# Splits of units 3, 6 and 9 ahead of GpSimd's wait for the next mask; halved mask loads, a three-part bfloat16 turn, and inverse sums of two groups widened in DRAM

## The chip, the cores and the metric

The kernel runs on one core of one Trainium2 chip. The metric is the device time of one execution in microseconds, from the runs' median. The engines of the core are TensorE (PE, its weight loads are PEld), VectorE (DVE), ScalarE (ACT), GpSimd (POOL) and SyncE (SP), each with a queue of its own that it works off in order; transfers go through 16 DMA engines.

## The reference, cut to what matters

```python
x = layernorm(x + self_attention(x))          # 1024 tokens, 16 heads of 8, one key/value head
x = layernorm(x + cross_attention(x, ctx, mask))   # 6404 context rows, 16 heads of 8
x = layernorm(x + experts(x))                 # top-1 of 8 experts, 128 x 128 each

# in both attentions, per head (the cross one with masked scores at -1e9)
scores = q @ k.T / sqrt(8)
out = softmax(scores) @ v
```

All inputs are float32. The mask is int32, 1024 x 6404; where it is 0 the score becomes -1e9, and here that is the same columns for every token: all but a tail of the context.

## The kernel before

**Units and steps.** Each attention is cut into 16 units: 8 pairs of heads times 2 halves of the tokens (512 each). A unit of self attention has 8 steps, one of cross attention has 10 (`SELF_U`, `NBLK`; `X(j, b)` is block b of cross unit j). The kernel keeps 1280 keys for the cross stage: the last 1024 and one chunk of 256 that the mask leaves alive. One step of the main loop does, on TensorE: two "column" products of keys and queries into an ST bank (L1539 in self, L1752 in cross), two "row" products of queries and keys into an RT bank (L1527, L1745), 16 steps ahead of the columns, and the products of probabilities and values of the step before (L1512, eight small matmuls). DVE takes the maximum of each RT bank (L944, L961, L962); ACT makes the exponentials of ST (L1309, L1298). RT has two banks, ST three; they go round in the order of `RT_AT` and `ST_AT`, in which extra jobs (`RT_JOBS`, `ST_JOBS`) take a bank each.

**Maxima.** A softmax needs its row maxima before its columns. When a unit's last row is reduced, DVE writes its maxima to `finx` (L938). GpSimd splits them in `split_max` (L566, L568) into a high and a low float32r part, `mxh`. TensorE turns `mxh` by a matmul with the identity (`turn_max`, L1490) three or five steps ahead of where the unit's columns begin (`TURN`), ACT copies the result to `mxr` (L1238), and SP sends it as rows of `Qs` (`max_rows`, issue at L317), where it is subtracted within the column products. TensorE waits for the split at the turn, and for the landing at the unit's first column (`have_max`).

**The mask.** GpSimd counts the mask in 16 pieces m (128 tokens x 3328 columns of int32, 1.7 MB each). Per piece it waits for the load, clamps it to bytes (L613), adds it to the counts (L622) and asks for piece m + 2 (`load_mask`, issue at L543). The splits stand in the same queue at fixed places: `MAX_AHEAD` says which split comes before the clamp of a piece, and so before the wait for its load, `MAX_BETWEEN` which comes between clamp and add. From the counts DVE finds the live chunk, which the cross stage needs.

**Sums.** The values' matmuls also give each head's sum of exponentials. They go out with the outputs to DRAM and come back as `den`, and the outputs as `aTr` (`o_back` on SP). There are four groups: s0, s1 (self, first and second half of the tokens), x0, x1. DVE inverts `den` (`sums_back`, L1050). TensorE spreads the inverses to all rows of a head with a selecting matrix (`spread`, L1600, an RT job); DVE multiplies (`spread_rows`, L1056, into `aT`); TensorE projects (`project_out`, L1608, another RT job); DVE adds it to `x` and takes the statistics (`residual`); GpSimd normalises (`normalise`); TensorE turns x and, in self, makes the cross queries. For s1 this stands at the steps `X(1, 3)` to `X(2, 6)`, for x0 at `X(9, 3)` to `X(10, 6)`.

**In Qs** each half of the partitions holds 32 rows of query products (`PRODUCTS`), two rows of maxima (`MAXROWS`) and one of the penalty.

## Time and profile before

| | us |
|---|---|
| median of 3 runs | 462.83 (462.34 to 463.98) |
| profiled execution | 465.59 |
| its span | 464.0 |
| TensorE, VectorE, ScalarE, GpSimd busy | 438.2, 395.0, 360.8, 248.7 |

Times in the profile are microseconds from the start of the span. A busy TensorE is not TensorE at its peak. A row of the timeline is one instruction, or several alike that follow each other (xN); in square brackets stands the idle time of its engine ahead of it and what ended that.

### The profile page before, as it was taken

Reading aid. Unit: us, or ns where it says so; the run is one execution under the profiler, and the core shown is the slowest. Engines: PE = TensorE matmul, PEld = TensorE weight load, DVE = VectorE, ACT = ScalarE, POOL = GpSimd, SP = SyncE. Lnnn points to the kernel's source line nnn. Section 1 sums busy time; section 2 is a strip of 40 time slices with the busy share of each in tenths; the row PEclk is TensorE's granted clock in tenths of the full one; section 3 lists DMA queues with packets and bytes.
Section 4 is the critical chain, followed back from the end, with each engine's and each line's share of the span. In section 5 each row is a group of like instructions: output and inputs, shape, how many; then the busy total and the mean of one; then the engine's idle time right before and its main releaser. Section 6 shows DMA issues by size and latency. Waiting matters only on the chain.

```text
span 464.0 us, 10785 instructions
## 1 busy us (share of the span) xinstructions
PE 438.2 (94%) x3873; PEld 177.2 (38%) x3873; DVE 395.0 (85%) x520; ACT 360.8 (78%) x708; POOL 248.7 (54%) x383
## 2 busy tenths in 40 slices
PE   7999999999889999999999999999999999999983
PEld 2543333333334333333344334333344443333441
DVE  5969989999788899899998999999999999941455
ACT  6338888889765877788868888889968888978723
POOL 4834889987897904042456644445447354320563
PEclk9879999999988999999999999999999999999978
DMA  6957967599770056221322346322212122110000
GB/s 164 342 121 230 310 201 293 182 364 350 249 316 1 15 114 98 64 68 42 92 71 69 115 92 105 89 72 60 83 45 69 49 72 70 47 32 23 4 24 26
DMA packets 24596, 56.08 MB, mean 121 GB/s; under 512 B 6442, under 2 KB 15928, under 8 KB 22492
## 3 DMA queue, kind: packets, MB, share of 16 engines
q0 software_dynamic: 7536, 37.91, 25.1%
q1 hardware_dynamic: 16424, 17.24, 14.3%
q8 instruction: 33, 0.54, 0.5%
q10 hardware_dynamic: 580, 0.20, 0.2%
q14 instruction: 23, 0.19, 0.1%
HBM read 45.60 MB, written 9.18 MB: 118 GB/s over the span
## 4 chain that ended last, share of the span: by engine, by line
PE 66%; DVE 12%; POOL 8%; DMA 7%; issue 4%; ACT 2%; SPq 0%; ACTq 0%; DVEq 0%; POOLq 0%
PE O L1512 25%; PE ST L1752 15%; PE RT L1745 7%; DVE mxs L944 7%; PE ST L1539 5%; POOL big L613 4%; DMA big<-in_mask 4%; PE RT L1527 3%; PE RT L1638 2%; DMA Qs<-mxr 2%; POOL big L622 2%; PE ST L1645 1%; PE O L1490 1%; DVE mxc L962 1%; PE RT L1608 1%
## 5 line engine op out<-in xcount | busy, mean ns | idle before, releaser
L1309 ACT ACTIVATE prob<-ST 128x512 f32<-128x512 f32 x512 | 279.5, 599 | 52.0 <-PE ST L1539 21.8
L944 DVE TENSOR_REDUCE mxs<-RT 128x2 f32<-128x1024 f32 x128 | 153.2, 1222 | 17.1 <-PE RT L1527 16.2
L961 DVE TENSOR_REDUCE mxc<-RT 128x2 f32<-128x1024 f32 x128 | 152.6, 1221 | 2.8 <-PE RT L1745 1.9
L1752 PE MATMUL ST<-Qs,Kc 64*128 64x512 f32 x320 | 117.4, 450 | 0.0
L1745 PE MATMUL RT<-Kr,Qs 64*128 64x512 f32 (+1 forms) x384 | 114.5, 398 | 0.0
L1512 PE MATMUL O<-prob,vst 128*9 128x256 f32 x1280 | 99.1, 381 | 1.7 <-ACT prob L1298 0.5
L1539 PE MATMUL ST<-Qs,Kself 64*128 64x512 f32 x256 | 96.2, 448 | 2.7 <-DMA Qs<-mxr 2.6
L1527 PE MATMUL RT<-Kself,Qs 64*128 64x512 f32 x256 | 89.8, 466 | 3.2 <-DVE mxs L944 2.0
L690 POOL DMA_DIRECT2D Kr<-kd x96 | 47.9, 503 | 72.7 <-PE RT L1745 57.6
L1512 PE MATMUL O<-prob,Vs 128*9 128x256 f32 x1024 | 80.5, 386 | 1.3 <-ACT osb L1246 0.3
L1752 PEld LDWEIGHTS ST<-Qs,Kc 64*128 64x128 f32 x320 | 50.4, 184 | 66.1 <-issue 38.3
L1539 PEld LDWEIGHTS ST<-Qs,Kself 64*128 64x128 f32 x256 | 39.5, 186 | 54.7 <-ACT prob L1309 39.2
L1745 PEld LDWEIGHTS RT<-Kr,Qs 64*128 64x128 f32 x384 | 51.3, 184 | 0.4 <-DVE mxc L961 0.4
L613 POOL TENSOR_SCALAR big<-big 128x3328 uint8<-128x3328 uint32 x16 | 47.4, 2961 | 6.5 <-DMA big<-in_mask 6.1
L700 POOL DMA_DIRECT2D Kc<-kd x64 | 31.6, 498 | 33.5 <-PE ST L1752 31.7
L962 DVE TENSOR_REDUCE mxc<-RT 128x4 f32<-128x1024 f32 x32 | 39.0, 1224 | 4.4 <-PE RT L1745 4.2
L1527 PEld LDWEIGHTS RT<-Kself,Qs 64*128 64x128 f32 x256 | 35.5, 189 | 11.7 <-DVE mxs L944 7.1
L1512 PEld LDWEIGHTS O<-prob,vst 128*9 128x9 f32 x1280 | 19.4, 88 | 53.1 <-ACT prob L1309 16.2
L1298 ACT ACTIVATE prob<-ST 128x512 f32<-128x512 f32 x64 | 34.8, 595 | 5.1 <-PE ST L1752 3.4
L1512 PEld LDWEIGHTS O<-prob,Vs 128*9 128x9 f32 x1024 | 15.8, 88 | 47.7 <-ACT prob L1309 33.4
L622 POOL TENSOR_TENSOR big<-big 128x832 int32<-128x832 int32 x14 | 27.5, 1962 | 0.8
L566 POOL CAST mxh<-finx 128x8 fp32r<-128x8 f32 x32 | 6.1, 191 | 34.6 <-DVE finx L938 34.5
(224 smaller groups left out, 331.8 us busy)
## 6 DMA issues: line engine op xcount, KB each, us to landing
big<-in_mask POOLq DMA_DIRECT2D x16, 1664.0 KB, 8.0
Kc<-kd POOLq DMA_DIRECT2D x64, 80.0 KB, 2.2
Kr<-kd POOLq DMA_DIRECT2D x64, 64.0 KB, 2.1
od_s<-osb SPq DMA_DIRECT2D x16, 128.0 KB, 2.6
kd<-Vx SPq DMA_DIRECT2D x4, 512.0 KB, 6.7
Qs<-qd_x SPq DMA_DIRECT2D x8, 256.0 KB
od_x<-osb SPq DMA_DIRECT2D x14, 128.0 KB, 1.7
Qs<-qd_s SPq DMA_DIRECT2D x12, 128.0 KB, 5.6
```

The lines of the kernel that those rows point to most:

```text
L613: g_.tensor_scalar(sums if q == 0 else dead8, maskI[m % 2].bitcast(U32), 1.0, 0.0, ALU.min, ALU.max) \
L622: g_.tensor_tensor(sums.bitcast(I32), sums.bitcast(I32), dead8.bitcast(I32), ALU.add) \
L690: pool.dma_start(Kr[r:r + PROD, w].bitcast(F32), head_rows(U, f)[:, w]).then_inc(S(f"kr{part}"), 16)
L944: freed(v.tensor_reduce(mxs[:, h % 2, c2, :].rearrange("p (f t) -> p f t", f=2)[:, :, q], bank[:, :].rearrange("p (f k) -> p f k", f=2), A ...
L961: return v.tensor_reduce(o[:, :, u % 4], src, AX.X, ALU.max)
L962: return v.tensor_reduce(o[:, :, 2 * (u - SRU):2 * (u - SRU) + 2], src.rearrange("p f (t k) -> p f t k", t=2), AX.X, ALU.max)
L1309: freed(nc.scalar.activation(prob[:, s % SLOTS, f * HALF:(f + 1) * HALF], bank[:, :], ACT.Exp))
L1512: mm = mmul(O[32 * q:32 * q + VW, 0:256], v[q // 2], prob[:, slot, q * 256:(q + 1) * 256], start=G is not None, stop=False, skip_group_che ...
L1527: mm = mmul(bank[:, f * HALF:(f + 1) * HALF], Qs[STACK[f], h, q * P:(q + 1) * P], Kself[STACK[f], c2 * 512:(c2 + 1) * 512], start=True, st ...
L1539: st_done(mmul(st_place((c, f))[:, :], Kself[STACK[f], b * P:(b + 1) * P], Qs[STACK[f], g, :], start=True, stop=True))
L1745: mm = mmul(o_, Qs[STACK[f], U, q * P:(q + 1) * P], Kr[STACK[f], w], start=True, stop=not gen, skip_group_check=True)
L1752: mm = mmul(o[:, :], Kc[STACK[f], b * P:(b + 1) * P], Qs[STACK[f], j, :], start=True, stop=not gen, skip_group_check=True)
```

## The change

- `MAX_AHEAD` and `MAX_BETWEEN`: the splits of units 3, 6 and 9 come ahead of the clamps of masks 3, 7 and 12 instead of behind them. The splits of units 4 and 8 stay between.
- `load_mask` asks for each piece in two halves of 1664 columns, both on the same semaphore.
- `split_max` makes three bfloat16 parts in four chained operations; `turn_max` multiplies them with a bfloat16 identity in one pass, 24 rows instead of 16; six rows of `Qs` take the maxima, so that the product rows move to 0 and 96.
- For s1 and x0 the inverses go from `rden` to DRAM (`inverses_out`) and come back repeated eight times as `rdenw` (`inverses_in`), both on SP. GpSimd multiplies `aTr` by it (in `norm_work`), so that spread and multiply leave TensorE and DVE. The projection comes four steps later, the normalisation and all that follows ten steps later. The second half's cross queries are gathered in two pairs of transfers instead of one, two and one.

```diff
-MAX_AHEAD = {0: 0, 2: 2, 6: 5, 9: 7, 14: 10}
-MAX_BETWEEN = {0: 1, 3: 3, 4: 4, 7: 6, 10: 8, 12: 9}
+MAX_AHEAD = {0: 0, 2: 2, 3: 3, 6: 5, 7: 6, 9: 7, 12: 9, 14: 10}
+MAX_BETWEEN = {0: 1, 4: 4, 10: 8}
...
-                pool.dma_start(maskI[m % 2], t["mask"][q * P:(q + 1) * P, w * HALFT:(w + 1) * HALFT]) \
-                    .then_inc(S(f"mask_in{m % 2}"), 16)
+                for c in range(0, HALFT, HALFT // 2):
+                    pool.dma_start(maskI[m % 2][:, c:c + HALFT // 2],
+                                   t["mask"][q * P:(q + 1) * P, w * HALFT + c:w * HALFT + c + HALFT // 2]) \
+                        .then_inc(S(f"mask_in{m % 2}"), 16)
...
-                g_.tensor_copy(mxh[:, :, 0, :], parts).then_inc(S("mx_part"), 1)
+                step(g_.tensor_copy(mxh[:, :, 0, :], parts))
+                step(g_.tensor_tensor(mxl[:, :, :], parts, mxh[:, :, 0, :], ALU.subtract))
+                g_.tensor_copy(mxh[:, :, 1, :], mxl[:, :, :]).then_inc(S("mx_part"), 1)
                 pool.wait_ge(S("mx_part"), G + 1)
-                g_.tensor_tensor(mxh[:, :, 1, :], parts, mxh[:, :, 0, :].bitcast(F32), ALU.subtract) \
+                g_.tensor_tensor(mxh[:, :, 2, :], mxl[:, :, :], mxh[:, :, 1, :], ALU.subtract) \
                     .then_inc(S("mx_split"), 1)
...
-                rows = mxh[:, :, :, :].bitcast(F32).rearrange("p f k t -> p (f k t)")
-                if bank is None:
-                    mm = mmul(O[0:16, 256:256 + P], rows, ident[:, :], start=False, stop=False, skip_group_check=True)
-                else:
-                    mm = nc.tensor.transpose(ST[bank][0:16, 0:P], rows, ident[:, :])
+                o = O[0:24, 256:256 + P] if bank is None else ST[bank][0:24, 0:P]
+                mm = mmul(o, mxh[:, :, :, :].rearrange("p f k t -> p (f k t)"), identb[:, :], start=bank is not None,
+                          stop=bank is not None, skip_group_check=True)
...
+            def inverses_out(a):
+                k = 1 if a == "s" else 2
+                sp.wait_ge(S("rden"), k + 1)
+                load(rd[a].rearrange("u q (h k) -> (u q h) k", k=P), rden[:, :], "rden_out")
+
+            def inverses_in(a):
+                k = 1 if a == "s" else 2
+                sp.wait_ge(S("rden_out"), 16 * k)
+                for q in range(4):
+                    w, r = slice((q % 2) * 256, (q % 2 + 1) * 256), 64 * (q // 2)
+                    load(rdenw[r:r + 64, w], rd[a][:, q, :].unsqueeze(1).to_broadcast([8, DH, 256]), "rden_in")
...
-                if j == 1:
+                if j in (1, 9):
+                    k = 1 + j // 8
+                    pool.wait_ge(S("o_back"), 64 * (k + 1))
+                    pool.wait_ge(S("rden_in"), 64 * k)
+                    pool.wait_ge(S("rt_ready"), number(RT_AT, ("s0 y", "s1 y")[k - 1]))
+                    g_.tensor_tensor(aT[:, :], aTr[:, :], rdenw[:, :], ALU.mult).then_inc(S("o_scaled"), 1)
+                if j == 2:
                     normalise("s", 1)
...
-                if s == X(1, 3):
-                    spread_rows("s", 1)
-                if s == X(1, 5):
+                if s == X(1, 9):
                     residual("s", 1)
```

GpSimd's queue around mask 3, before: the clamp (TENSOR_SCALAR) of mask 3, split 3 (the two rows with mxh), the add, and the load of mask 5.

```order
L613 TENSOR_SCALAR big<-big 128x3328
L566 CAST mxh<-finx 128x2x4
L568 TENSOR_TENSOR mxh<-finx,mxh 128x2x4
L622 TENSOR_TENSOR big<-big 128x832
L543 DMA big<-in_mask 128x3328
```

And in the changed kernel:

```order
L592 CAST mxh<-finx 128x2x4
L593 TENSOR_TENSOR mxl<-finx,mxh 128x8
L594 CAST mxh<-mxl 128x2x4
L596 TENSOR_TENSOR mxh<-mxl,mxh 128x2x4
L641 TENSOR_SCALAR big<-big 128x3328
L650 TENSOR_TENSOR big<-big 128x832
L568 DMA big<-in_mask 128x1664 x2
```

The split has moved ahead of the clamp, has four operations, and the load is two.

TensorE's queue at step `X(1, 3)`, before: the last row products of the step, the spread of s1, and the values.

```order
L1752 MATMUL ST<-Qs,Kc 128x512
L1745 MATMUL RT<-Kr,Qs 128x256 x2
L1600 MATMUL RT<-rden,sel 128x128 x4
L1512 MATMUL O<-prob,vst 9x256 x4
```

In the changed kernel there is no such matmul, and the projection of s1 stands at `X(1, 9)`, two steps behind the unit's turn:

```order
L1521 MATMUL O<-identb,mxh 24x128
...
L1785 MATMUL ST<-Qs,Kc 128x512
L1778 MATMUL RT<-Kr,Qs 128x512
L1641 MATMUL RT<-wo_s,aT 128x128 x4
L1542 MATMUL O<-prob,vst 9x256 x4
```

The projection was ahead of the turn of its unit and is behind it now.

SP's queue in the changed kernel from the maxima of unit 17 on; before, it had neither the row with rd_s<-rden nor the one with rdenw.

```order
L321 DMA Qs<-mxr 6x4x128
L321 DMA rd_s<-rden 64x128
L321 DMA od_x<-osb 128x256
L321 DMA big<-in_we 128x1024
L321 DMA rdenw<-rd_s 64x1x256 x4
L321 DMA Qs<-mxr 6x4x128
```

The five added transfers stand between the maxima of two units.

## Rows read from the trace of the kernel before

**Rows 1.** The page's busy times: engine, us (share of the span), instructions.

```profile
PE 438.2 (94%) x3873; PEld 177.2 (38%) x3873; DVE 395.0 (85%) x520; ACT 360.8 (78%) x708; POOL 248.7 (54%) x383
```

**Rows 2.** The timeline of TensorE: start, us, engine, line, operation, what, xcount.

```profile
60.76 0.49 PE L1539 MATMUL ST<-Qs,Kself 64*128 64x512 f32 x1
61.97 0.50 PE L1539 MATMUL ST<-Qs,Kself 64*128 64x512 f32 x1
...
78.15 0.50 PE L1539 MATMUL ST<-Qs,Kself 64*128 64x512 f32 x1
79.56 0.49 PE L1539 MATMUL ST<-Qs,Kself 64*128 64x512 f32 x1
```

**Rows 3.** Waits, who <- for whom: us in total, times, longest us.

```profile
POOL big L613 <- DMA big<-in_mask: 6.1, 4, 2.4
...
PE ST L1539 <- DMA Qs<-mxr: 2.6, 2, 1.5
...
PE O L1490 <- POOL mxh L568: 2.3, 3, 1.8
```

**Rows 4.** One stretch: its length, busy us (instructions) by engine, granted clock, DMA.

```profile
136.00:142.00 6.00, 6.00 (x35) 3.20 (x33) 3.14 (x3) 2.29 (x5) 5.75 (x3) 0.50 0.26 103
```

**Rows 5.** The timeline of GpSimd in the mask stretch, columns as in rows 2.

```profile
53.25 2.96 POOL L613 TENSOR_SCALAR big<-big 128x3328 uint8<-128x3328 uint32 x1 [1.85 <-DMA big<-in_mask]
56.16 0.19 POOL L566 CAST mxh<-finx 128x8 fp32r<-128x8 f32 x1
56.43 0.20 POOL L568 TENSOR_TENSOR mxh<-finx,mxh 128x8 fp32r<-128x8 f32 x1
56.60 1.96 POOL L622 TENSOR_TENSOR big<-big 128x832 int32<-128x832 int32 x1
58.50 0.59 POOL L543 DMA_DIRECT2D big<-in_mask  x1
...
65.48 0.19 POOL L566 CAST mxh<-finx 128x8 fp32r<-128x8 f32 x1 [2.19 <-DVE finx L938]
...
76.66 0.19 POOL L566 CAST mxh<-finx 128x8 fp32r<-128x8 f32 x1 [0.72 <-DVE finx L938]
...
125.62 0.60 POOL L543 DMA_DIRECT2D big<-in_mask  x1 [1.79 <-DMA Qs<-mxr]
...
134.69 0.20 POOL L568 TENSOR_TENSOR mxh<-finx,mxh 128x8 fp32r<-128x8 f32 x1
```

**Rows 6.** The timeline of VectorE: the maxima of unit 3.

```profile
55.20 0.17 DVE L938 TENSOR_REDUCE finx<-mxs 128x8 f32<-128x16 f32 x1
```

**Rows 7.** GpSimd's issues by line: ns min/median/max, first and last start; time to landing.

```profile
L543 POOL DMA_DIRECT2D big<-in_mask x16: 558/592/812, 9.3 to 131.2; - x16
...
DMA to landing us min/median/max: 6.6/8.0/14.3
L690 POOL DMA_DIRECT2D Kr<-kd x96: 496/498/615, 181.2 to 395.0; - x96
```

**Rows 8.** The timeline of the cross stage at a turn.

```profile
265.98 0.20 POOL L568 TENSOR_TENSOR mxh<-finx,mxh 128x8 fp32r<-128x8 f32 x1
...
266.50 0.31 PEld L1490 LDWEIGHTS O<-ident,mxh 128*16 128x16 f32 x2
...
267.02 0.50 PE L1752 MATMUL ST<-Qs,Kc 64*128 64x512 f32 x1
```

**Rows 9.** The timeline of TensorE around the spread of s1.

```profile
231.97 0.49 PE L1752 MATMUL ST<-Qs,Kc 64*128 64x512 f32 x1
...
234.59 0.50 PE L1752 MATMUL ST<-Qs,Kc 64*128 64x512 f32 x1
```

**Rows 10.** Timelines of VectorE and GpSimd; groups by line, busy us, mean ns.

```profile
227.47 0.93 DVE L1050 RECIPROCAL rden<-den 64x128 f32<-64x128 f32 x1
...
238.59 0.26 POOL L708 COPY vst<-Vx 128x90 f32<-128x90 f32 x1 [1.25 <-PE O L1512]
...
L575 POOL TENSOR_TENSOR xq_low<-xq_full,xq_high 128x512 f32<-128x512 f32 x2 | 2.6, 1280 | 2.5 <-ACT xq_full L1261 2.5
```

More of the change, by code:

```diff
@@ L37 @@
 STACK = (slice(0, 64), slice(64, P))
-PRODUCTS = (1, 64 + 3)
-MAXROWS = slice(0, 100, 33)
+PRODUCTS = (0, 96)
+MAXROWS = slice(36, 87, 10)
 PENROWS = (34, 65)
@@ L75 @@
 RT_JOBS = {76: ("s0 spread",), 79: ("s0 y",), 94: ("count",), 99: ("flags",), KV - 1: ("km",),
-           X(1, 3): ("s1 spread",), X(1, 5): ("s1 y",), X(9, 3): ("x0 spread",), X(9, 5): ("x0 y",),
-           X(10, 6): ("x0 logits",), X(14, 6): ("e0",), X(15, 1): ("e1",),
+           X(1, 9): ("s1 y",), X(9, 9): ("x0 y",),
+           X(11, 6): ("x0 logits",), X(14, 6): ("e0",), X(15, 1): ("e1",),
            STEPS: ("x1 spread", "x1 y", "x1 logits", "e2", "e3", "u7")}
 ST_JOBS = {66: ("bias",), 86: ("s0 turn",), 88: ("s0 q",), KV: ("vm",),
-           X(2, 3): ("s1 turn",), X(2, 6): ("s1 q",), X(10, 3): ("x0 turn",),
+           X(3, 3): ("s1 turn",), X(3, 6): ("s1 q",), X(11, 3): ("x0 turn",),
            STEPS: ("c0", "u0", "u1", "b0", "u2", "u3", "x1 turn", "u4", "c1", "u5", "b1", "u6")}
@@ L189, in decoder_layer @@
         finx = sb("finx", [P, QT])
-        mxh = sb("mxh", [P, 2, 2, 4], F32R)
-        mxr = sb("mxr", [16, 2, P])
+        mxl = sb("mxl", [P, 2, 4])
+        mxh = sb("mxh", [P, 2, 3, 4], BF16)
+        identb = sb("identb", [P, P], BF16)
+        mxr = sb("mxr", [24, 2, P])
         osb = sb("osb", [P, 2, 256])
         aTr, aT = sb("aTr", [P, HALF]), sb("aT", [P, HALF])
+        rdenw = sb("rdenw", [P, HALF])
         den, rden = sb("den", [64, P]), sb("rden", [64, P])
@@ L251, in decoder_layer @@
         qd = {a: dram(f"qd_{a}", [2, DH, HEADS, Q]) for a in "sx"}
+        rd = {a: dram(f"rd_{a}", [8, 4, 256]) for a in "sx"}
         kd, pd = dram("kd", [HEADS, PROD, KPAD]), dram("pd", [1, KUSE])
@@ L358, in o_back @@
                     sp.wait_ge(S(f"o_in{par}"), 16 * (4 * (k - 1) + units // 2))
-                if k > 1:
-                    before = ("s0", "s1", "x0")[k - 2]
-                    sp.wait_ge(S("rt_free"), number(RT_AT, before + " spread"))
+                if k == 2:
+                    sp.wait_ge(S("rt_free"), number(RT_AT, "s0 spread"))
+                if k > 2:
+                    sp.wait_ge(S("o_scaled"), k - 2)
                 g0 = 8 * ph
@@ L390, in gather_x_queries @@
                     sp.wait_ge(S("xq_in"), 80 * ph)
-                load(Qs[MAXROWS, 8 * ph:8 * ph + 8, :].bitcast(F32).rearrange("o h q -> o (h q)"), zerof[:, :], "xq_in")
+                load(Qs[MAXROWS, 8 * ph:8 * ph + 8, :].bitcast(F32).rearrange("o h (t q) -> o (h t) q", q=P),
+                     zerof[0:6, :].unsqueeze(1).to_broadcast([6, 32, P]), "xq_in")
                 for k in parts:
@@ L889, in _ @@
                 mark(v.tensor_reduce(rowc[:, f, 1:2], ident[:, r + 2 * DH:r + PROD], AX.X, ALU.add))
-                mark(v.tensor_tensor(rowc[:, f, 2:3], ident[:, 66 * f:66 * f + 1], ident[:, 66 * f + 33:66 * f + 34],
-                                     ALU.add))
+                r = MAXROWS.start + 3 * MAXROWS.step * f
+                mark(v.tensor_reduce(rowc[:, f, 2:3], ident[:, r:r + 21:10], AX.X, ALU.add))
                 mark(v.tensor_reduce(rowc[:, f, 3:4], parts[:, :, 0, :], AX.XY, ALU.add))
@@ L1236, in max_copy @@
                     act.wait_ge(S(f"max_in{G % 2}"), 16 * (G // 2))
-                turned = O[0:16, 256:256 + P] if bank is None else ST[bank][0:16, 0:P]
+                turned = O[0:24, 256:256 + P] if bank is None else ST[bank][0:24, 0:P]
                 nc.scalar.copy(mxr[:, G % 2, :], turned).then_inc(S("mx_copied"), 1)
@@ L1605, in project_out @@
                 o = rt_place(f"{a}{ph} y")
-                pe.wait_ge(S("rt_free"), number(RT_AT, f"{a}{ph} spread"))
+                if NORMS[a, ph] in (2, 3):
+                    pe.wait_ge(S("o_scaled"), NORMS[a, ph] - 1)
+                else:
+                    pe.wait_ge(S("rt_free"), number(RT_AT, f"{a}{ph} spread"))
                 for q in range(4):
@@ L1884, in cross @@
                             row(r, 1 - f)
[L1885 to L1887 removed]
+                    if s == X(1, 9):
                         project_out("s", 1, wo_s)
[L1889 to L1891 removed]
+                    if s == X(9, 9):
                         project_out("x", 0, wo_x)
[L1893 removed]
+                    if s == X(11, 6):
                         logits(0)
```

53 lines of the change are left out of this document (26 added, 27 removed).

## The prediction, made before the changed kernel ran

> **What bounds the kernel now.** I read the busy shares first, then TensorE's timeline, then the waits, then GpSimd's timeline. TensorE is busy 438.2 us, 94% of the span [rows 1], so it sets the pace nearly everywhere. One step of the self stage takes 61.97 - 60.76 = 1.21 us; the step with the turn of the maxima in it takes 79.56 - 78.15 = 1.41 us, so a turn costs TensorE 0.20 us [rows 2]. Where TensorE does wait in the self stage, two causes stand out: 2.6 us for the transfer of turned maxima into Qs (twice, up to 1.5) and 2.3 us for GpSimd's split (three times, up to 1.8) [rows 3]. The 1.8 is the turn of unit 10, at 134.9, and 1 us behind it the granted clock is at half: 1.2 GHz instead of 2.4 [rows 4]. Six us at half clock do the work of three, but TensorE also waits there, so I put the loss at 2.5 us.
>
> Between 50 and 145 GpSimd runs masks and splits in one fixed queue, with little idle time; four waits for mask data sum to 6.1 us [rows 3]. The question is whether that queue has room for what the change adds.
>
> **Splits and halved loads: the GpSimd queue.** Per mask it now does a clamp of 2.96, an add of 1.90 to the issue, and an issue; a split takes 56.60 - 56.16 = 0.44, its second operation starting 0.27 behind its first [rows 5]. The change makes three additions.
> - A split has four chained operations instead of two: + 2 x 0.27 = 0.54.
> - A mask load is two issues. One issue is 0.59 whatever it carries [rows 7], so + 0.6 per mask. Bounds: 0 if only the rows' bytes count, 0.6 if the issue does. I take 0.6, since an issue of 32 short rows takes 0.50 too [rows 7].
> - Split 3 goes ahead of mask 3. Its maximum is complete at 55.20 + 0.17 = 55.37 [rows 6], while mask 3's data came at 53.25 and the clamp ran before the split [rows 5]. Now the clamp waits: 55.43 + 1.0 = 56.4 instead of 53.25, + 3.1, less 0.1 because TensorE's cheaper turns bring the maximum forward: + 3.0.
>
> Up to the end of split 10, which was at 134.69 + 0.20 = 134.9 [rows 5], this adds 3.0, eleven second issues (masks 5 to 15) 6.6, and seven splits (4 to 10) 3.8: 13.4 us. The idle time that can take it up is 2.19 and 0.72 for maxima and 1.79 for a landing [rows 5], and of the 6.1 for masks the 4.3 behind mask 3 [rows 3 and 5]: 9.0. I take it that all of it is used, because the time between a load and its use grows by more than these waits. The end of split 10 so moves by + 4.4, to 139.3.
>
> TensorE loses its own earlier waits on the way (the 2.6 for landings should go: the halved packets let the small transfer in sooner, and GpSimd's loads lie further apart), but wins nothing by it, since it then waits at turns 5, 7 and 10 for splits that are late. For turn 5: mask 5's clamp starts at about 72.0, so split 5 ends at 79.9. TensorE wants it at 77.5: a wait of 2.4. Turn 7 is about as late, turn 10 later still. So unit 10's turn sets the time: **+ 4.4**. The half clock behind it comes again. A half clock after turn 5 or 7 delays only the next maxima; GpSimd would wait 1.5 for maximum 6, and I count half of that: **+ 0.7**.
>
> Moving splits 6 and 9 ahead costs nothing: their maxima are by then complete when the queue gets there, and either order would hold the same work.
>
> One rule of the Trainium skill speaks against the halving (DMA: Bandwidth & Descriptors, section Bandwidth: batch transfers to at least 1 MiB; a half mask is 832 KB). By that page's formula, 2.0 us + bytes / 436 KB per us, an estimate gives 5.9 us for a whole mask and 7.9 for two halves strictly one behind the other, + 2.0 per mask. The trace has 6.6 to 14.3 us to the landing of a whole one [rows 7], and the halves overlap, so the sum leaves this out.
>
> **The three-part bfloat16 turn on TensorE.** Two passes of a float32 matmul become one bfloat16 pass. The 0.20 of a turn falls to between 0 and 0.20; I take 0.07, a gain of 0.13, because a pass of a quarter of the columns' work should leave little but its weight load. Turn 10 itself gives **- 0.1**. Units 11 to 16 have slack ahead of the turn: 6 x 0.13 = 0.8, less 0.5 at the third wait for a split of [rows 3], unit 15, where the longer split shows in full: **- 0.3**. In the cross stage the split ends at 265.98 + 0.20 = 266.18 and TensorE loads it at 266.50, the next step starting at 267.02 [rows 8]. With 0.54 more the split ends at 266.72, 0.2 late. The next step then starts at 266.72 plus load and pass. If that is half of the former 0.52, 266.98; if an eighth, 266.79. I take a gain of 0.1: 15 x 0.1, **- 1.5** (bounds: - 3.5 and + 3.3).
>
> **The inverse sums through DRAM.** The spread of s1 makes a step 234.59 - 231.97 = 2.62 us instead of 1.21 [rows 9]. Its four matmuls and the wait for their bank go: - 1.4, and x0's the same: **- 2.8** (bounds - 2.4 and - 2.8). The projection stays and comes four steps later. What replaces it must be in time. The reciprocals of group s1 are at 227.47 + 0.93 [rows 10]; SP sends them out behind the maxima of that unit, about 2 us to land, then issues four widening loads of about 0.6 each, so rdenw is full by about 235. GpSimd reaches its multiply behind the copy of V at 238.59 + 0.26 and needs 1.3 us, as for a like subtraction [rows 10]: 240.1. The projection then comes two steps behind the turn of that unit, at about 241.9. So some 1.8 us cover the multiply; if that cover is gone, TensorE waits, 1 us at the worst. The loads lie in SP's queue ahead of the next unit's maxima, which are ready only five steps after them: nothing. The second half's queries are now asked for in two pairs; between the last pair's issue and the first row that needs it lie six steps, 7.3 us, for 512 KB: nothing, or 1 us at the worst. GpSimd's normalisation moves on by a unit, behind the statistics instead of waiting for them, which frees the queue and no one else.
>
> **The sum.** 4.4 + 0.7 - 0.1 - 0.3 - 1.5 - 2.8 = + 0.4, on the profiled execution's 465.59 us (464.0 of span, 1.6 around it). That execution was 2.76 above the median of the runs. So 462.83 + 0.4 = **463.2**.
>
> **Rivals.**
> - Faster: the second issue costs GpSimd nothing. Then 6.6 of the 13.4 is missing, split 10 ends 2.2 earlier than before instead of 4.4 later, and the time is 463.2 - 6.6 = **456.6**. For it speaks only that one descriptor list twice as long might be what 0.59 pays for; against it, that 0.59 stands for 128 rows as 0.50 does for 32. The Trainium skill (same page, section SWDGE vs HWDGE vs iDMA) has each transfer engine alternate between the queues. By that, small transfers gain from halved packets, which the sum counts as hidden behind GpSimd; in this rival it would show.
> - Slower: the late operand in the cross stage. If load and pass take the former 0.52 from 266.72, each of 15 steps starts at 267.24 instead of 267.02: + 3.3 in place of - 1.5, so **468.0**. It decides at 0.30 us from the split's end to the next step. Against it: one pass instead of two. For it: the first pass is fixed cost, weight load and start, and the trace has no bfloat16 turn.
> - The halved loads don't let the small transfers in: TensorE then still waits at unit 8's rows, but GpSimd's queue is later anyway; the same 463.2.
>
> **How the numbers follow.** Forecast (with the third rival) 0.58, its own range 460.5 to 465.7: no half clock at all would take 2.5 off, half clocks with a GpSimd wait each would add 2. The faster rival has 0.23, the slower one 0.19. A measurement can tell 0.3%, 1.4 us, from no change. Of the forecast 0.10 lies below 461.4, 0.38 within, 0.10 above 464.2. So faster 0.33, same 0.38, slower 0.29. Range 456.5 to 467.5.
>
> **What would show it.** In the changed kernel's GpSimd timeline: clamp 3 at about 56.4 and none of the four waits for masks behind it; two issues of 0.6 per mask; split 10 ending near 139. In TensorE's waits: those for landings gone, those for splits grown to 8 us or more, at turns 5, 7 and 10. In the cross stage: the step behind a turn at 1.3 instead of 1.4, with a short wait for the split. No RT spread matmuls but two. A queue that ends before 135 proves the first step wrong, a cross unit longer than 12.6 us the third.

## The result, and the profile after

| | before | changed |
|---|---|---|
| median of 4 runs each | 462.58 (459.35 to 463.98) | 470.15 (469.33 to 471.65) |
| profiled execution (span) | 465.59 (464.0) | 469.91 (468.3) |
| TensorE, VectorE, ScalarE, GpSimd busy | 438.2, 395.0, 360.8, 248.7 | 433.2, 390.9, 359.9, 272.6 |

The changed kernel is slower: ratio 1.0159, 95% interval 1.0115 to 1.0203. It lies outside the range that I gave. In a later set of runs (`changed_again` below), 12 more of the changed kernel against 30 of the kernel before gave 1.0104 (1.0070 to 1.0138), median 468.18 against 463.41. So the loss is 5 to 7.5 us. Runs of one program scatter (31 of the kernel before, in one set, lie between 458.87 and 473.77 us, at mean granted clocks from 0.984 down to 0.957); all ratios and intervals leave out runs more than 1.5% above the fastest of their kernel, while the medians keep them.

The busy times are the first clue. TensorE and VectorE have less to do than before [rows 1], as the change meant; GpSimd has 24 us more. The page's busy line of the changed kernel:

```profile
PE 433.2 (93%) x3826; PEld 172.0 (37%) x3826; DVE 390.9 (83%) x518; ACT 359.9 (77%) x708; POOL 272.6 (58%) x466
```

Its waits of TensorE (who <- for whom: us, times, longest), against [rows 3]: those for the split have grown from 2.3 to 12.0, those for landings have stayed.

```profile
PE O L1521 <- POOL mxh L596: 12.0, 4, 6.7
PE ST L1569 <- DMA Qs<-mxr: 2.2, 2, 1.3
```

TensorE's timeline at the turns of units 5, 7 and 10 (start, us, what, [idle before]):

```profile
79.75 0.23 PE L1521 MATMUL O<-identb,mxh 128*24 128x128 bf16 x1 [1.71 <-POOL mxh L596]
...
102.56 0.28 PE L1521 MATMUL O<-identb,mxh 128*24 128x128 bf16 x1 [2.85 <-POOL mxh L596]
...
141.99 0.28 PE L1521 MATMUL O<-identb,mxh 128*24 128x128 bf16 x1 [6.69 <-POOL mxh L596]
```

GpSimd's timeline of the changed kernel, against [rows 5]: split 3 and the clamp of mask 3, the pair of issues, the three waits that are left, and the last operation of split 10 (which began at 134.69 before).

```profile
55.50 0.19 POOL L592 CAST mxh<-finx 128x8 bf16<-128x8 f32 x1 [4.14 <-DVE finx L972]
...
56.31 0.20 POOL L596 TENSOR_TENSOR mxh<-mxl,mxh 128x8 bf16<-128x8 f32 x1
56.49 2.96 POOL L641 TENSOR_SCALAR big<-big 128x3328 uint8<-128x3328 uint32 x1
59.53 1.97 POOL L650 TENSOR_TENSOR big<-big 128x832 int32<-128x832 int32 x1
61.44 1.13 POOL L568 DMA_DIRECT2D big<-in_mask  x2
...
107.42 1.12 POOL L568 DMA_DIRECT2D big<-in_mask  x2
...
117.54 2.96 POOL L641 TENSOR_SCALAR big<-big 128x3328 uint8<-128x3328 uint32 x1 [2.03 <-DMA big<-in_mask]
...
125.25 2.95 POOL L641 TENSOR_SCALAR big<-big 128x3328 uint8<-128x3328 uint32 x1 [0.64 <-DMA big<-in_mask]
...
131.10 1.13 POOL L568 DMA_DIRECT2D big<-in_mask  x2 [0.85 <-DMA Qs<-mxr]
...
141.74 0.20 POOL L596 TENSOR_TENSOR mxh<-mxl,mxh 128x8 bf16<-128x8 f32 x1
```

Where in the program the time is lost can be read from one instruction that comes once per unit, the last reduction of the unit's maxima into `finx` on VectorE. Those of unit 11, 12 and 31 in the kernel before:

```profile
146.06 0.17 DVE L938 TENSOR_REDUCE finx<-mxs 128x8 f32<-128x16 f32 x1
158.12 0.17 DVE L938 TENSOR_REDUCE finx<-mxs 128x8 f32<-128x16 f32 x1
...
408.76 0.17 DVE L938 TENSOR_REDUCE finx<-mxc 128x8 f32<-128x16 f32 x1 [0.23 <-DVE mxc L989]
```

and in the changed kernel:

```profile
153.56 0.17 DVE L972 TENSOR_REDUCE finx<-mxs 128x8 f32<-128x16 f32 x1
165.45 0.17 DVE L972 TENSOR_REDUCE finx<-mxs 128x8 f32<-128x16 f32 x1
...
413.17 0.17 DVE L972 TENSOR_REDUCE finx<-mxc 128x8 f32<-128x16 f32 x1 [0.23 <-DVE mxc L1023]
```

Up to unit 11, the end of the mask stretch, the changed kernel has lost 7.5 us. From there to unit 31 it wins 3.1 back, and the spans differ by 4.3. I use these rows, one per unit, for every kernel below, and call the two parts the mask stretch (to unit 11) and the rest.

The 7.5 has two parts. Turn 10 starts 7.05 us later (141.99 for 134.94), within 0.1 us of the end of split 10 in both kernels. From there to unit 11 it is 11.57 us instead of 11.12. Both of these stretches run largely at half clock; in kernels below whose clock stays full there it is 8.4 to 9.2 us.

### The profile page after: what moved, and what is told of

Its sections match the earlier page's. It is cut to its first block, busy times and chain, and to the rows that moved or that the text cites. A ratio compares the mean times of both kernels' runs of the same rounds, so it can differ in the third digit from the quotient of the medians.

```text
span 468.3 us, 10780 instructions
## 1 busy us (share of the span) xinstructions
PE 433.2 (93%) x3826; PEld 172.0 (37%) x3826; DVE 390.9 (83%) x518; ACT 359.9 (77%) x708; POOL 272.6 (58%) x466
## 4 chain that ended last, share of the span: by engine, by line
PE 60%; DVE 13%; POOL 12%; DMA 6%; issue 5%; ACT 2%; SPq 0%; POOLq 0%; DVEq 0%; ACTq 0%
PE O L1542 22%; PE ST L1785 13%; DVE mxs L978 7%; PE RT L1778 6%; PE ST L1569 5%; POOL big L641 4%; DMA Qs<-mxr 4%; PE RT L1557 3%; DVE mxc L995 2%; POOL big L650 2%; PE RT L1671 2%; POOL big L568 2%; PE ST L1678 1%; DMA Kc<-kd 1%; DVE mxc L996 1%
## 5 line engine op out<-in xcount | busy, mean ns | idle before, releaser
L1557 PE MATMUL RT<-Kself,Qs 64*128 64x512 f32 x256 | 91.3, 469 | 2.9 <-DVE mxs L978 1.7
L592 POOL CAST mxh<-finx 128x8 bf16<-128x8 f32 x32 | 6.2, 193 | 34.7 <-DVE finx L972 34.7
```

What stands on the lines that cost most here:

```text
L1557: mm = mmul(bank[:, f * HALF:(f + 1) * HALF], Qs[STACK[f], h, q * P:(q + 1) * P], Kself[STACK[f], c2 * 512:(c2 + 1) * 512], start=True, st ...
```

## The experiments

All ratios are against the kernel before in the same set of runs; each kernel has 6 to 12 runs, the kernel before 23 to 31 in a set. In the five sets the median of before was 463.84, 463.19, 464.35, 463.41 and 463.10. The last three columns are from the one profiled execution: when split 10 ends, how long it is from the start of turn 10 to unit 11's `finx`, and when that `finx` starts (u11). One execution carries scatter of its own: unit 1 alone starts up to 2.4 us apart in kernels with the same code up to there.

| kernel | median us | ratio (95% interval) | split 10 ends | turn 10 to u11 | u11 |
|---|---|---|---|---|---|
| before | 462.58 | 1 | 134.89 | 11.12 | 146.06 |
| changed | 470.15 | 1.0159 (1.0115 to 1.0203) | 141.94 | 11.57 | 153.56 |
| whole_loads | 464.25 | 1.0034 (0.9985 to 1.0083) | 139.49 | 8.36 | 147.91 |
| whole_padded | 469.01 | 1.0129 (1.0074 to 1.0184) | 140.98 | 10.98 | 152.01 |
| halved_only | 465.86 | 1.0069 (1.0030 to 1.0108) | 141.24 | 8.69 | 149.98 |
| bf16_turn | 466.04 | 1.0062 (1.0013 to 1.0111) | 138.56 | 8.67 | 147.29 |
| inverse_dram | 461.30 | 0.9975 (0.9930 to 1.0021) | 136.70 | 9.64 | 146.40 |
| bf16_inverse | 464.12 | 0.9984 (0.9944 to 1.0025) | 137.61 | 8.67 | 146.33 |
| old_tables | 469.01 | 1.0176 (1.0118 to 1.0234) | 142.38 | 8.36 | 150.80 |
| tables_only | 467.42 | 1.0118 (1.0063 to 1.0174) | 135.61 | 11.13 | 146.79 |
| split3_only | 462.21 | 0.9980 (0.9943 to 1.0017) | 134.75 | 9.18 | 143.98 |
| splits69_only | 468.38 | 1.0074 (1.0038 to 1.0109) | 137.12 | 11.14 | 148.31 |
| waits_filled | 470.02 | 1.0126 (1.0055 to 1.0196) | 142.68 | 8.36 | 154.15 |
| split10_early | 460.27 | 0.9938 (0.9902 to 0.9973) | 132.55 | 9.22 | 142.44 |
| changed_early | 467.81 | 1.0100 (1.0041 to 1.0159) | 140.15 | 8.78 | 149.52 |
| bf16_inverse_early | 462.85 | 1.0001 (0.9971 to 1.0031) | 139.14 | 9.22 | 149.57 |
| splits_9_10_early | 458.54 | 0.9888 (0.9839 to 0.9937) | 133.02 | 9.23 | 142.91 |
| bf16_9_10_early | 462.17 | 1.0003 (0.9965 to 1.0041) | 137.69 | 12.23 | 149.97 |
| split6_ahead_too | 462.13 | 0.9962 (0.9919 to 1.0005) | 135.81 | 12.52 | 148.38 |
| changed_again | 468.18 | 1.0104 (1.0070 to 1.0138) | 143.52 | 9.49 | 153.07 |

In 15 of these 20 traces turn 10 starts 0.04 to 0.06 us behind the end of split 10, so GpSimd sets its time. The other five are waits_filled (turn 10 at 145.79, behind its zeros) and split10_early, changed_early, bf16_inverse_early and splits_9_10_early, where split 10 is done before TensorE gets there. Where the clock is full behind turn 10, u11 follows it by 8.36 to 9.23 us; where it is at half for all or part of that stretch, by 9.49 to 12.52.

### The halved loads: GpSimd's time or the smaller packets?

`whole_loads` is the changed kernel with one transfer per mask.

```diff
-                for c in range(0, HALFT, HALFT // 2):
-                    pool.dma_start(maskI[m % 2][:, c:c + HALFT // 2], ...)
+                pool.dma_start(maskI[m % 2], ...)
```

> The changed kernel with each mask asked for in one transfer again; all else as changed. Theory Q (GpSimd's queue is the path through the mask stretch, and its second issues are its largest part): eleven second issues of 0.53 us are gone up to split 10, 5.8 us; split 10 ends near 141.9 - 5.8 = 136.1 unless waits for mask data come back (up to 4), TensorE's longest wait for a split falls from 6.7 to 1 to 4 us, and the time is 470.2 - 5.8 = 464 (up to 467 if the waits for masks come back). Rival O (the order is the cause: split 3 ahead of mask 3): stays at 469 to 471. Rival C (the half clock around turn 10 is the cause and depends on the wait's length): the half clock falls back to 7 us and the time to 462.

464.25, 1.0034: by the ratios 5.8 us under the changed kernel of the first result, 3.2 under `changed_again`, where the intervals overlap. The number is that of theory Q, GpSimd's queue, but the way there is not quite. Split 10 ends 2.45 us earlier than in the changed kernel, not 5.8, because waits for masks came back (3.8 us in four). TensorE's wait at turn 10 is 2.35 us instead of 6.69, the clock stays full behind it, and that gives 11.57 - 8.36 = 3.2 us more at u11. And the halving changes two things, the second issue on GpSimd and the size of the packets. `whole_padded` keeps the packets whole and gives GpSimd the time back:

```diff
+                step(g_.tensor_copy(spare[:, :], onesf[:, 0:1].to_broadcast([P, 400])))
```

> The changed kernel with whole mask loads, and behind each of them a copy of 128x400 on GpSimd that nobody uses, meant to take the time of the second issue (0.53 us; a copy of 128x1024 took 1.05 and one of 128x128 0.30, so 0.5 to 0.6). It tells the two parts of the halving apart: GpSimd's time and the smaller packets. If GpSimd's time is the loss: back to the changed kernel's ratio to before, 1.013 to 1.018, 469 to 471. If the smaller packets are: as whole_loads, 1.003, 464 to 465. If the smaller packets even helped: above 471.

Its GpSimd timeline behind mask 3 shows the pad at the length of a second issue:

```profile
60.59 0.59 POOL L568 DMA_DIRECT2D big<-in_mask  x1
61.19 0.53 POOL L570 COPY spare<-onesf 128x400 f32<-128x400 f32 x1
```

469.01, 1.0129: the loss is back with whole packets, and so are the later split 10 (140.98) and the half clock behind turn 10. So the halving costs by GpSimd's time, 0.53 us behind each mask, in part directly and in part by the half clock that comes with it; these runs show no part for the packets. `halved_only` is the kernel before with the halving alone.

> The kernel before with halved mask loads alone. If the second issues are the main loss: eleven of 0.53 us make 5.8 us, of which the four waits for masks (6.1 us) take a part; TensorE's wait at turn 10 grows from 1.8 to 4 or more, and the time is 466 to 469. If they cost only together with the longer split: 463 to 464. If the halves let small transfers in sooner: the 2.6 us of waits for landings are gone, 461.

1.0069, some 3 us, just under what I expected for the issues as main loss: alone, part of the 5.8 us is still taken up. The long wait is not at turn 10, as I had written (0.35 there), but at turn 9, 4.88 us; split 10 ends 6.35 us later than before. Its waits for landings are 1.4 us once, against 2.6 in two before [rows 3], so the smaller packets can have brought about 1 us.

### The bfloat16 turn and the inverses, each alone

`bf16_turn` is the kernel before with the new `split_max` and `turn_max` (and `PRODUCTS`, `MAXROWS`, `mxh`, `mxr` as in the diff of the change) and nothing else.

> The kernel before with the three-part bfloat16 turn alone (four operations in a split, one pass in a turn, six rows of maxima). Theory Q: seven splits add 3.8 us to GpSimd's queue, which its four waits for masks (6.1 us) take up, so split 10 is at most 1 us later; TensorE gains 0.17 at each of 5 turns behind unit 10 and 0.09 at each of 15 cross turns: 462.6 - 2.0 + 0.5 = 461. Rival L (the splits between clamp and add are each late for TensorE): turns 5, 7 and 10 wait longer by their own 0.54 and what is ahead of them, 464.

1.0062, 466.0: not Q, whose split 10 was to be at most 1 us later; it ends 3.7 later. Nearer to rival L, which had named turns 5, 7 and 10. TensorE's timeline has where it is:

```profile
125.68 0.23 PE L1498 MATMUL O<-identb,mxh 128*24 128x128 bf16 x1 [3.18 <-POOL mxh L575]
```

That is turn 9 (0.30 of waiting before). In the rest it is as forecast: unit 16 stands 1.3 us later than before, unit 31 level with it. The gain of 1.3 us in the cross stage is there, and the mask stretch takes it and more: u11 is 1.2 us later although the clock is full behind turn 10, which it was not before.

`inverse_dram` is the kernel before with the inverses of s1 and x0 through DRAM and the norm's work moved with them.

> The kernel before with the inverses of groups s1 and x0 through DRAM alone, and the norm's work moved with it. Prediction's sum: two spreads of 1.4 us gone, 462.6 - 2.8 = 459.8. Rival: the spread's step was not on TensorE's path alone, or the later projection, normalisation and queries wait for GpSimd or for gathered rows: a gain of 0 to 1, 461.6 to 462.6.

461.30, 0.9975, not told apart from no change. The trace says more: from unit 17 to unit 31 it gains 1.8 us on before (from 0.4 behind to 1.4 ahead), not 2.8; the three later kernels built on it gain the same 1.8 there. TensorE's timeline at s1, the starts of the steps:

```profile
232.33 0.50 PE L1776 MATMUL ST<-Qs,Kc 64*128 64x512 f32 x1
...
233.55 0.50 PE L1776 MATMUL ST<-Qs,Kc 64*128 64x512 f32 x1
...
235.98 0.49 PE L1776 MATMUL ST<-Qs,Kc 64*128 64x512 f32 x1
...
237.88 0.49 PE L1776 MATMUL ST<-Qs,Kc 64*128 64x512 f32 x1
```

The spread's step is 1.22 instead of 2.62 [rows 9], - 1.40. The projection's step, four steps on, is 2.51 instead of 2.61. But the step from 235.98 to 237.88, with the unit's turn in it, is 1.90 where it was 1.41. In the changed kernel it is the same, and VectorE's timeline there is closed:

```profile
242.08 1.23 DVE L995 TENSOR_REDUCE mxc<-RT 128x2 f32<-128x1024 f32 x1 [0.39 <-issue]
243.22 0.16 DVE L972 TENSOR_REDUCE finx<-mxc 128x8 f32<-128x16 f32 x1
243.30 5.83 DVE L995 TENSOR_REDUCE mxc<-RT 128x2 f32<-128x1024 f32 x5
```

VectorE reduces a bank in 1.17 us where TensorE needs 1.21 for one; after the end of a unit it is behind, and TensorE's load for the row products waits 0.32 us for it in that step. Before, TensorE's long steps gave it the time. So the group gives 1.40 + 0.10 - 0.49 = 1.0, and two groups 2.0 at most.

`bf16_inverse` has both, which is the changed kernel with whole loads and the old places.

> The changed kernel with whole mask loads and the old places of the splits, so the bfloat16 turn and the inverses through DRAM alone. If the single parts add up: 0.6 - 0.25 = 0.4% above before, 465. If the new places cost something beside whole loads too: whole_loads' 1.003 less 0.2 to 1.0, 459 to 463. If the new places help a longer split: above 465.

0.9984: the parts add up within the intervals (1.0062 and 0.9975), and beside whole_loads the new places cost 0.5%, which these two do not tell from nothing. Its wait is at turn 9, 5.20 us:

```profile
124.69 0.28 PE L1519 MATMUL O<-identb,mxh 128*24 128x128 bf16 x1 [5.20 <-POOL mxh L594]
```

### The new places of the splits

`old_tables` is the changed kernel with the old tables, `tables_only` the kernel before with the new ones.

```diff
-MAX_AHEAD = {0: 0, 2: 2, 3: 3, 6: 5, 7: 6, 9: 7, 12: 9, 14: 10}
-MAX_BETWEEN = {0: 1, 4: 4, 10: 8}
+MAX_AHEAD = {0: 0, 2: 2, 6: 5, 9: 7, 14: 10}
+MAX_BETWEEN = {0: 1, 3: 3, 4: 4, 7: 6, 10: 8, 12: 9}
```

> The changed kernel with the splits of units 3, 6 and 9 between clamp and add again, as before. Theory Q: clamp 3 starts 3.0 us earlier, at 53.4, and all behind it; some of this goes into waits for mask data, so split 10 ends 1.5 to 3.0 us earlier and the time is 467.2 to 468.7. Rival O: the order is the whole loss, 462 to 464. A third: moving the splits of units 6 and 9 behind the clamp makes turn 7 or turn 9 later, and nothing is won: 470.

> The kernel before with the splits of units 3, 6 and 9 ahead of the clamps alone. If split 3 ahead costs what I wrote (clamp 3 is 3.0 us later): 1 to 3 us at turn 10 and 463.8 + 2 = 466. If the waits for masks take it up: 463.8.

Against what I had written, the old places win nothing in the changed kernel (1.0176), while the new ones cost the kernel before 1.2%. The one trace of tables_only does not show that cost: its u11 is only 0.7 us later than before, and the profiled execution of before was itself 3.0 us over its median. In old_tables, turn 9 waits where turn 10 did, 3.45 us, behind clamp 12 and its wait for data:

```profile
128.41 0.28 PE L1521 MATMUL O<-identb,mxh 128*24 128x128 bf16 x1 [3.45 <-POOL mxh L596]
```

The places were then tried apart on the kernel before: split 3 alone, and splits 6 and 9.

```diff
-MAX_AHEAD = {0: 0, 2: 2, 6: 5, 9: 7, 14: 10}
-MAX_BETWEEN = {0: 1, 3: 3, 4: 4, 7: 6, 10: 8, 12: 9}
+MAX_AHEAD = {0: 0, 2: 2, 3: 3, 6: 5, 9: 7, 14: 10}
+MAX_BETWEEN = {0: 1, 4: 4, 7: 6, 10: 8, 12: 9}
```

> The kernel before with split 3 alone ahead of the clamp of mask 3. If its 3.0 us of GpSimd waiting is what the new places cost: the same as tables_only, 1.009 to 1.015 of before. If it is split 6 or 9: 0.998 to 1.003.

> The kernel before with splits 6 and 9 alone ahead of the clamps of masks 7 and 12. My prediction's 'costs nothing': 0.998 to 1.002 of before, 463 to 465. If they are what tables_only showed (a split ahead can wait for its maximum while the mask is there, and moves the next load): 1.006 to 1.012.

This turns my two steps round. Split 3 ahead makes GpSimd wait 4.04 us at 53.6, and costs nothing (0.9980), though TensorE waits 4.83 us at turn 9. Splits 6 and 9 ahead, which I had put at nothing, cost 0.7%. GpSimd's timeline of splits69_only at split 6:

```profile
86.12 0.19 POOL L566 CAST mxh<-finx 128x8 fp32r<-128x8 f32 x1 [1.63 <-DVE finx L938]
86.56 2.96 POOL L613 TENSOR_SCALAR big<-big 128x3328 uint8<-128x3328 uint32 x1
```

Its maximum is not complete when the queue gets there, 1.63 us too early, with mask 7 ready. `split6_ahead_too` (below) has this place alone beside a good one for split 9.

### Is it the half clock?

Behind turn 10 the granted clock is at half, 1.2 GHz, as before [rows 4], and for longer. A window of the changed kernel (length, busy us by engine, granted clock, DMA):

```profile
139.50:149.50 10.00, 7.51 (x41) 3.92 (x45) 3.20 (x4) 2.94 (x7) 9.52 (x8) 0.53 0.42 172
```

Theory C: TensorE's waits bring the half clock, and that costs on top. `waits_filled` has TensorE work through the waits, on zeros that it adds to a part of its bank where they change nothing.

```diff
+            def fill(n):
+                for i in range(n):
+                    mmul(O[0:24, 256:512], wcol[:, 32:56], identb[:, :].unsqueeze(1).to_broadcast([P, 2, P]),
+                         start=False, stop=False, skip_group_check=True)
+
             def turn_max(G, bank=None):
+                fill({5: 14, 7: 28, 10: 56}.get(G, 0))
```

> The changed kernel; ahead of the turns of units 5, 7 and 10 TensorE gets 14, 28 and 56 matmuls of zeros by 256 columns (about 0.11 us each at full clock: 1.5, 3 and 6 us) that add nothing to any result, so that it works where the changed kernel's trace shows it waiting 2 to 6.7 us for the split. Theory C (TensorE's waits bring stretches of half clock, and these cost on top of the waits): the mean granted clock rises from 0.961 to 0.970 or more, and by the slope of time against clock in the 31 runs of the kernel before (5.3 us for 0.01) the time falls to 464 to 466. Theory Q (only GpSimd's lateness costs): the same 470, or 1 to 2 above it, since the zeros stand in TensorE's queue. Rival: the clock falls for something else than the waits: clock 0.961, time 470.

From 50 to 156 us the changed kernel and then waits_filled (behind the busy times: granted clock, DMA share, GB/s):

```profile
50.00:156.00 106.00, 92.92 (x858) 33.97 (x855) 87.41 (x93) 78.37 (x157) 92.42 (x97) 0.94 0.70 237
```

```profile
50.00:156.00 106.00, 101.99 (x962) 42.17 (x956) 88.42 (x92) 78.77 (x157) 93.04 (x95) 0.97 0.72 240
```

TensorE is busy 9 us more, and the mean clock of the runs is 0.973, against 0.961 in the first four of the changed kernel and 0.967 in `changed_again`. The time does not move, 470.02, and u11 is 154.15 for 153.56. GpSimd is as busy and as late as before. That looks as if the half clock cost nothing. The timelines say otherwise; GpSimd's split 10, then TensorE's zeros and its turn 10, then a window behind it:

```profile
142.48 0.20 POOL L596 TENSOR_TENSOR mxh<-mxl,mxh 128x8 bf16<-128x8 f32 x1
```

```profile
139.68 6.28 PE L1518 MATMUL O<-identb,wcol 128*24 128x256 bf16 x56
145.79 0.22 PE L1527 MATMUL O<-identb,mxh 128*24 128x128 bf16 x1
```

```profile
146.00:154.00 8.00, 7.72 (x69) 3.83 (x68) 6.67 (x6) 5.68 (x11) 6.59 (x3) 1.00 0.06 19
```

The zeros for turn 10 were too many: they held TensorE for 3.1 us after the split was done. Behind them the clock is full, and from turn 10 to u11 it is 8.36 us instead of 11.57, 3.2 less. The two cancel. The half clock also came in another place, from 125.6 to 132.4 behind turn 9, which had no zeros and waited 2.68 us. So this experiment does not part the theories by its time. What parts them is the stretch from turn 10 to u11: 8.36 us in all of whole_loads, old_tables and waits_filled, at full clock, and 11.57 in the changed kernel, at half. By the Trainium skill (TensorE: Matmul & The Clock Gate, section Terms) the penalty is about the throttled time by one minus the granted share; by that rule the 10.2 us at half clock (140.0 to 150.2) would cost an estimated 5.1 us. The traces have 3.2: for the first 2 us of it TensorE stood waiting, and a step then took 2.12 us instead of 1.21, not twice as long.

The kernel before has the half clock too. With the same turn and steps, halved_only has 8.69 us at full clock where before has 11.12: 2.4 us, near my 2.5 (1.9 by split3_only, 9.18). So the half clock behind turn 10 costs 3.2 us in the changed kernel's trace and 2.4 in the one before, and theory C explains little of the difference between them; GpSimd's 7.05 us explain most.

### Repairs: what if split 10 and split 9 stand where they can be early?

Ahead of split 10 GpSimd makes two copies into Vx, 2.7 us, that nobody waits for so soon.

```diff
-MAX_AHEAD = {0: 0, 2: 2, 6: 5, 9: 7, 14: 10}
+MAX_AHEAD = {0: 0, 2: 2, 6: 5, 9: 7}
...
                 if m == 13:
+                    split_max(10)
                     pool.wait_ge(S("q_out"), 64)
```

`split10_early` has this on top of inverse_dram, `changed_early` on top of the changed kernel (with its tables), `bf16_inverse_early` on top of bf16_inverse.

> The kernel before with the inverses through DRAM, and with split 10 ahead of GpSimd's two copies into Vx (2.7 us) instead of behind them. Theory C: the wait at turn 10 (1.9 us) and the half clock behind it go: 461.3 - 2 to 4 = 457 to 459, clock 0.98 or more. Rival: another wait (unit 8's or 9's landing) brings the half clock anyway: 461.

> The changed kernel, halved loads and all, with split 10 ahead of the two copies into Vx. By theory Q split 10 ends near 141.9 - 2.7 = 139.2, TensorE's 6.7 us at turn 10 become 4.0, and the time falls by 2.7: 467. Rival: with turn 10 earlier nothing else is bound by GpSimd and all 6.7 go: 463.5.

> As bf16_inverse, with split 10 ahead of GpSimd's two copies into Vx. If turn 10 is what the longer split makes late: about 1% under bf16_inverse and, with the cross turns' 1.2 us less, level with split10_early or below it: 0.990 to 0.994 of before, 459 to 461. Rival: turn 9 is late in its place (four splits are 0.54 longer each), and it stays above split10_early: 0.996 or more.

split10_early is at 0.9938, faster than before; u11 is at 142.44, 4.0 us under inverse_dram. TensorE's clock still drops once in it, behind a landing, so the rival was half right. changed_early has 467.81, near the 467 of theory Q, but its ratio of 1.0100 does not tell it from `changed_again`, 1.0104; split 10 ends 1.8 us earlier, not 2.7. bf16_inverse_early gains nothing over bf16_inverse: turn 9 is where that one waited already, and it still does, 6.20 us.

```profile
127.94 0.28 PE L1520 MATMUL O<-identb,mxh 128*24 128x128 bf16 x1 [6.20 <-POOL mxh L594]
```

Split 9 stands there behind the clamp of mask 12 and the wait for its data. The last three kernels move it ahead of that wait, which is one entry of the change's own tables.

```diff
-MAX_AHEAD = {0: 0, 2: 2, 6: 5, 9: 7}
-MAX_BETWEEN = {0: 1, 3: 3, 4: 4, 7: 6, 10: 8, 12: 9}
+MAX_AHEAD = {0: 0, 2: 2, 6: 5, 9: 7, 12: 9}
+MAX_BETWEEN = {0: 1, 3: 3, 4: 4, 7: 6, 10: 8}
```

> The kernel before with the inverses through DRAM, split 10 ahead of the two copies into Vx and split 9 ahead of the clamp of mask 12. If turn 9 was late because its split stood behind a wait for mask data (1.39 us and 2.95 of clamp in inverse_dram, where TensorE waited 1.89 there): under split10_early's 0.994, 0.988 to 0.992, 457 to 459. Rival: nothing, 0.994.

458.54, 0.9888: the lowest median here, 1.1% under the kernel before and 2.1 to 2.7% under the changed one; its interval overlaps that of split10_early. Its GpSimd timeline: split 9 fits into the time in which mask 12 is not there yet, and split 10 ends at 133.0 instead of 134.9 (132.6 in split10_early).

```profile
119.01 0.20 POOL L585 CAST mxh<-finx 128x8 fp32r<-128x8 f32 x1
119.30 0.20 POOL L587 TENSOR_TENSOR mxh<-finx,mxh 128x8 fp32r<-128x8 f32 x1
120.00 2.95 POOL L632 TENSOR_SCALAR big<-big 128x3328 uint8<-128x3328 uint32 x1 [0.50 <-DMA big<-in_mask]
...
132.82 0.20 POOL L587 TENSOR_TENSOR mxh<-finx,mxh 128x8 fp32r<-128x8 f32 x1
```

Two more start from it: with the bfloat16 turn, and with split 6 ahead of the clamp of mask 7 (`7: 6` moved from the second table to the first).

> splits_9_10_early with the three-part bfloat16 turn in addition. TensorE has 0.1 us less at each of 15 cross turns and 0.17 at each self turn (1.2 us less behind unit 11 in bf16_turn's trace); GpSimd has 0.54 more in each of seven splits among the masks, 3.8 us. If both splits stand where their lengthening is covered: 0.985 of before, 456.5. If GpSimd's queue takes more than the turns give, as in bf16_turn and bf16_inverse_early: 0.992 to 1.000, 460 to 463.

> splits_9_10_early with split 6 ahead of the clamp of mask 7 in addition, the one place of the change that is not in split3_only (no cost) or in splits_9_10_early (a gain). GpSimd would wait for maximum 6 ahead of a mask that is there (1.63 us in splits69_only). If that is what the new places cost: 0.5 to 1% above splits_9_10_early, 461 to 463. If it was split 9's place beside a late turn 10: no difference, 458.5.

The bfloat16 turn takes all of the gain away, 1.0003: split 10 ends 4.7 us later than in splits_9_10_early (four operations instead of two in seven splits make 3.8), the half clock is back behind turn 10, and the cheaper pass gives TensorE less than that. Split 6 ahead takes 0.7% (0.9962 against 0.9888; the intervals overlap slightly), the same as splits 6 and 9 cost the kernel before. In its trace split 10 ends 2.8 us later, and the half clock is back here too. Since split 9's place lost nothing (0.9888 after 0.9938, a gain of 0.5% that the intervals don't secure and the traces don't show), split 6's is the likely carrier of that cost.

`changed_again` is the changed kernel, unaltered.

> The changed kernel once more, beside the others of this call: 1.013 to 1.019 of before, 469 to 472, if nothing but the programs differs between the calls.

1.0104, a little less than expected; the first result had four runs of it. All parts above are to be held against 1.010 to 1.016. Its trace confirms the mask stretch (split 10 ends at 143.52, u11 is 7.0 us later than before) but not the rest: it gives back 0.2 us of that by unit 31, where the first trace gave back 3.1. TensorE waits 1.19 us for a landing at 303.06 (unit 23), and the clock is at half from 379.3 to 382.6 (unit 29).

## Why the prediction was wrong

**What held.** The start of clamp 3 (56.4 expected, 56.49 measured), the second issue (0.6 expected, 1.13 for the pair less 0.60), the 0.27 per operation of the split, the late turns 5, 7 and 10, the self turns behind unit 10 (0.3 expected, 0.4 between units 11 and 15), the cross turns (1.5 expected, 1.3 measured; step 1.43 instead of 1.53), and, in the paragraph on what bounds the kernel, the 2.5 us for the half clock (2.4 by halved_only). The two rivals did not come. The faster one needed a free second issue. The slower one's 468.0 is near the measured time, but by chance: its late operand did come in most cross turns (the split of the unit at 323.8 ends at 323.59 and TensorE's load waits for it), yet load and pass took 0.21 us to the next step, under the 0.30 that was to decide.

```profile
323.64 0.09 PEld L1521 LDWEIGHTS O<-identb,mxh 128*24 128x24 bf16 x1 [0.38 <-POOL mxh L596]
```

**The step that failed: "I take it that all of it is used".** I let 9.0 us of GpSimd's idle time take up 13.4 us of additions. In the trace of the changed kernel the additions are 3.0 for split 3, 11 x 0.53 = 5.8 for the issues, 7 x 0.54 = 3.8 for the splits, 12.6 in all. But 2.03 + 0.64 + 0.85 = 3.5 us of idle time are left, so only 5.5 were used: 12.6 - 5.5 = 7.1. Measured, split 10 ends at 141.94 instead of 134.89, 7.05 later (8.6 in `changed_again`). That is the + 4.4 that should have been + 7.

Which waits were used up and which stayed tells why. The 2.9 us for maxima went whole, and 0.9 of the 1.79 for a landing; the waits for masks behind mask 3 gave only 1.6 of their 4.3. GpSimd asks for mask 11 itself, after the add of mask 9. If GpSimd is late at that point, the load is late by as much, and its wait is not shortened. Only what stands between a load's issue and its use can take a wait up. The kernel before, from the issue for mask 11 to its clamp:

```profile
103.42 0.59 POOL L543 DMA_DIRECT2D big<-in_mask  x1
104.66 2.95 POOL L613 TENSOR_SCALAR big<-big 128x3328 uint8<-128x3328 uint32 x1 [0.65 <-DMA big<-in_mask]
...
112.93 2.96 POOL L613 TENSOR_SCALAR big<-big 128x3328 uint8<-128x3328 uint32 x1 [2.42 <-DMA big<-in_mask]
```

In between GpSimd is idle for 0.65 + 2.42 = 3.07 us. In the changed kernel the pair for mask 11 starts at 107.42, its second half at about 108.0, and the clamp at 117.54: 9.5 us, as long as before. In these 9.5 us stand one second issue and one longer split more, 0.53 + 0.54 = 1.07 us, and the idle time is 2.03, 1.04 less. I had written that this time "grows by more than these waits" without putting the 1.07 beside the 3.07. A wait for a maximum is another matter, since VectorE does not start later for GpSimd's sake: split3_only adds a wait of 4 us early and loses nothing, and in its trace the waits for maxima 4 and 5, 2.19 and 0.72 before [rows 5], are gone.

**"+ 0.7" for half clocks behind turns 5 and 7.** It rested on a wait of GpSimd for maximum 6. GpSimd was too late for it, and there is none in the trace (0.40 in `changed_again`): this term is nothing. What it stood beside, the stretch behind turn 10, is 0.45 longer than before.

**"Moving splits 6 and 9 ahead costs nothing."** Wrong for 6. I held that the maxima are complete when the queue gets there. Split 6's is not while GpSimd is on time (1.63 us in splits69_only); in the changed kernel GpSimd was so late that there is no such wait in its trace, which fits that old_tables found no gain. Split 9's place costs nothing where split 10 is early as well; a gain is not shown.

**"The 2.6 for landings should go."** They are 2.2 in the changed kernel and did not matter there, since the turns set the time. That is the third rival, at no price, as I had put it.

**The spreads, - 2.8.** The mechanism was right, the term too large: 1.0 for a group instead of 1.4, and 1.8 over both (1.75 to 1.79 in four traces). The 0.4 goes into the next turn's step, which becomes VectorE's (1.90 us for 1.41). I had named no engine that would be late next, though VectorE's 85% [rows 1] was there to read.

**The sum.** Mask stretch + 7.5 instead of + 5.1; the rest - 3.1 instead of - 4.7. Together + 4.3 for + 0.4, on the profiled executions. The medians differ by 7.6 in the first set of runs and by 4.8 in the later one. The spans of `changed_again` and before differ by 5.1, since the rest gave back less there. What is left of the 7.6 no trace here shows; the kernel before's profiled execution was 3.0 us over its median.

**The parts.** Of 5 to 7.5 us the halving is 3.2 to 5.8 (whole_loads), by GpSimd's time and the half clock that it brings. The bfloat16 turn is some 3 on the kernel before, and 1.1% in bf16_9_10_early. Split 6's place costs up to 0.7% where GpSimd is on time, nothing in the changed kernel. The inverses give 1 to 2. The parts do not add up to the whole, because they use the same idle time; how much each has beside the others was tried only for the halving, and by how much it is the lateness and by how much the clock only in single traces.

## What to carry to other kernels

Slack in a queue that issues its own loads is not a sum of its waits: a wait for data takes up only the work that is added between that load's last issue and its use. Filling an engine's wait to keep its clock up is a test only if the filling ends before the wait does. When work is taken off the engine that sets the pace and put on the engine that it waits for, price each added instruction there, the DMA issues too. A short step that another engine waits for goes ahead of a wait for data if its input is then complete, and behind it if not; the trace's idle bracket at that step says which.
